# One sweep of probability-value products per step in place of two, in an audio-tower kernel

## What is computed

```
h = relu(patches @ W1 + b1) @ W2 + b2
h = h + bitlinear_attention(layernorm(h))     # 16 heads of 16
h = h + one_expert_ffn(layernorm(h))          # capacity 100
h = h + real part of a complex decaying scan(layernorm(h))
h = h + mixture_of_8_experts(layernorm(h))    # two of 8 experts for each row
```

```
scores = einsum('bhqd,bhkd->bhqk', q, k) * SCALE
attn = softmax(scores, axis=-1)
out = einsum('bhqk,bhkd->bhqd', attn, v)
```

## Time and profile before

| | |
|---|---|
| three executions | 504.51, 506.26, 506.55 us; median 506.26 us |
| the profiled execution | 505.15 us, with a span of 503.4 us |
| mean granted clock of TensorE | 0.954 of full speed |
| busy: PE, DVE, ACT, POOL | 439.5, 281.0, 206.0, 166.6 us |
| the chain that ended last | PE 65%, DVE 17% |

### The profile page before, as it was taken

How to read it: one execution, slowest core, us unless ns; L and a number is a source line. 1 busy time by engine, 2 the same in 40 slices (tenths; PEclk the granted TensorE clock), 3 DMA queues, 4 the chain that set the end, 5 groups by cost and what they waited for, 6 DMA issues and landing times.

```text
span 503.4 us, 9416 instructions
## 1 busy us (share of the span) xinstructions
PE 439.5 (87%) x3418; PEld 282.7 (56%) x3419; DVE 281.0 (56%) x853; ACT 206.0 (41%) x385; POOL 166.6 (33%) x140
## 2 busy tenths in 40 slices
PE   0889899798778856878899999999999999999991
PEld 0545456456455645646557666666666666566651
DVE  0498786686869999998975767346411111111110
ACT  1234653463587424246426632453333333333330
POOL 6051010010101044631434455443544442554322
PEclk9999999999967956898999999999999999999997
DMA  8999210046045100732005222341333225333211
GB/s 174 255 210 211 58 40 3 9 132 241 19 155 210 44 7 1 276 143 85 26 28 126 42 43 43 101 69 20 50 46 53 42 42 187 63 45 50 41 21 21
DMA packets 36103, 43.16 MB, mean 86 GB/s; under 512 B 5216, under 2 KB 30560, under 8 KB 35904
## 3 DMA queue, kind: packets, MB, share of 16 engines
q1 hardware_dynamic: 26384, 32.14, 22.9%
q0 software_dynamic: 7488, 10.23, 12.9%
q10 hardware_dynamic: 2192, 0.27, 0.5%
HBM read 30.96 MB, written 11.53 MB: 84 GB/s over the span
## 4 chain that ended last, share of the span: by engine, by line
PE 65%; DVE 17%; issue 5%; DMA 5%; ACT 4%; SPq 3%; POOLq 0%; DVEq 0%; ACTq 0%
PE psum L2257 26%; PE psum L2276 13%; PE psum L1874 9%; DMA M3s<-in_x_dram 4%; PE psum L2267 3%; PE psum L1888 3%; PE psum L1900 2%; PE psum L2247 2%; PE psum L1918 2%; DVE st_att L1028 1%; SPq L316 1%; DVE H L1271 1%; DVE qtok L1188 1%; DVE Eb L1068 1%; DMA out_dram<-O,dst_i 1%
## 5 line engine op out<-in xcount | busy, mean ns | idle before, releaser
L1771 DVE TENSOR_TENSOR QT<-QT,psum 128x512 f32<-128x512 f32 x39 | 26.8, 687 | 136.9 <-PE psum L2257 136.9
L2276 PE MATMUL psum<-M3s,KT 128*128 x312 | 74.1, 380 | 1.3 <-ACT KT L822 0.8
L2257 PE MATMUL psum<-M1s,KT 128*128 x156 | 74.0, 597 | 1.1 <-issue 0.8
L2257 PE MATMUL psum<-M2s,KT 128*128 x156 | 73.3, 592 | 0.0
L2276 PEld LDWEIGHTS psum<-M3s,KT 128*128 128x128 f32 x312 | 58.6, 190 | 22.1 <-issue 16.1
L833 ACT ACTIVATE O<-psum,gate_slot 128x256 f32<-128x256 f32 x39 | 18.5, 474 | 106.7 <-PE psum L2276 106.7
L1874 PE MATMUL psum<-M2s,M1s 128*128 128x512 f32 x128 | 58.7, 602 | 0.8 <-ACT H L688 0.7
L503 POOL DMA_INDIRECT KT<-mixture_rows_in,src_i x39 | 42.6, 1093 | 33.0 <-issue 19.7
L2257 PEld LDWEIGHTS psum<-M2s,KT 128*128 128x128 f32 x156 | 29.6, 190 | 37.3 <-issue 37.3
L530 POOL DMA_INDIRECT mixture_rows_out<-O,src_i x17 | 30.8, 1813 | 33.1 <-ACT O L833 13.3
L818 ACT ACTIVATE QT<-psum 128x512 f32<-128x512 f32 x39 | 23.3, 596 | 39.8 <-PE psum L2257 39.7
(11 more groups left out here) (407 smaller groups left out, 747.1 us busy)
## 6 DMA issues: line engine op xcount, KB each, us to landing
M3s<-in_x_dram SPq DMA_DIRECT2D x4, 1024.0 KB, 11.8
M3s<-in_L_ffn_W_dram SPq DMA_DIRECT2D x1, 4096.0 KB, 15.1
M2s<-in_L_ffn_W_dram SPq DMA_DIRECT2D x1, 4096.0 KB, 15.4
M1s<-in_L_ffn_W_dram SPq DMA_DIRECT2D x1, 4096.0 KB, 15.1
M3s<-in_x_dram SPq DMA_DIRECT2D x4, 992.0 KB, 15.7
M1s<-vtok SPq DMA_DIRECT2D x64, 34.0 KB, 1.9
mixture_rows_out<-H SPq DMA_DIRECT2D x4, 512.0 KB, 4.1
M1s<-in_L_tok_W_dram SPq DMA_DIRECT2D x2, 512.0 KB, 14.2
```

Of the source, the lines that this page charges most:

```text
L1771: v.tensor_tensor(sil[:, u, :], sil[:, u, :], bank[3], ALU.mult).then_inc(v_gated, 1)
L2257: last = mm(z, xrT[:, u, c, :], w[:, bass.ds(e, 1), c, :].rearrange("p a h -> p (a h)"), start=(c == 0), stop=(c == CH - 1))
L2276: last = mm(bank[6][:, 0:DM], actT[:, u, c, :], M3s[:, bass.ds(e, 1), c, :].rearrange("p a d -> p (a d)"), start=(c == 0), stop=(c == HC - 1))
```

## The change

There are five buffers of probabilities (`turned`): the two of `Eb`, the two of `PT` and 512 numbers of each partition of `M1s` that nothing used at that time. Batch `b` has its scores in `EB[b]` (the two of `Eb`, in turn, as before) and its transposed probabilities in `PB[b]`: `PT` 0, `PT` 1, the part of `M1s`, and for batch 3 `Eb` 0, which batch 2 has by then given up. `values` is called once for a step, over all four batches for each head, at the place of the second call.

```
+        turned = [Eb[:, 0], Eb[:, 1], PT[:, 0], PT[:, 1], part(M1s, VX_W + STRIDE * DM + CH * SN, NH * 32)]
+        turned = turned[0:4] + [turned[4].rearrange("p (h k) -> p h k", k=32)]
+        EB = [turned[k] for k in (0, 1, 0, 1)]
+        PB = [turned[k] for k in (2, 3, 4, 0)]
...
-                    a.activation(Eb[:, b % 2], Eb[:, b % 2], ACT.Exp).then_inc(a_exp, 1)
+                    a.activation(EB[b], EB[b], ACT.Exp).then_inc(a_exp, 1)
...
-            act.wait_ge(v_probsT, BT * STEPS)
+            act.wait_ge(p_values, BT * STEPS)
             norm(SR, 0, X4[0], v_norm4_in, a_norm4)
...
-            act.wait_ge(p_values, BT * STEPS)
             norm(SR, 1, X4[1], v_norm4_in, a_norm4)
...
                 wait(dve, v_probsT, BT * i + b - 1)
+                if b == 0:
+                    wait(dve, p_values, BT * i)
...
-                v.tensor_tensor(Eb[:, b % 2], score_rows(b), m, ALU.subtract).then_inc(v_less_max, 1)
+                v.tensor_tensor(EB[b], score_rows(b), m, ALU.subtract).then_inc(v_less_max, 1)
...
             def turn(i, b):
                 dve.wait_ge(a_exp, BT * i + b + 1)
-                wait(dve, p_values, BT * i + b - 1)
-                v.transpose(PT[:, b % 2].rearrange("p h k -> p (h k)"), Eb[:, b % 2].rearrange("p h k -> p (h k)")
+                wait(dve, p_values, BT * i)
+                if b == BT - 1:
+                    dve.wait_ge(v_probsT, BT * i + b)
+                v.transpose(PB[b].rearrange("p h k -> p (h k)"), EB[b].rearrange("p h k -> p (h k)")
                             ).then_inc(v_probsT, 1)
...
-            def values(i, slot, batches):
+            def values(i, slot):
...
-                pe.wait_ge(v_probsT, BT * i + batches[-1] + 1)
+                pe.wait_ge(v_probsT, BT * (i + 1))
                 for h in range(NH):
                     w = TS * VW
-                    for b in batches:
+                    for b in range(BT):
                         last = mm(bank[2 + h // 4][32 * b:32 * b + 32, w * (h % 4):w * (h % 4 + 1)],
-                                  PT[:, b % 2, h, :], Vx[:, b, :, h, :], start=True, stop=True)
-                last.then_inc(p_values, len(batches))
+                                  PB[b][:, h, :], Vx[:, b, :, h, :], start=True, stop=True)
+                last.then_inc(p_values, BT)
...
-            values(0, 2, range(0, 2))
             layer2(2)
-            values(0, 2, range(2, BT))
+            values(0, 2)
...
             att_proj(0)
-            values(1, 3, range(0, 2))
             pe.wait_ge(v_att_added, 1)
             layer2(3)
-            values(1, 3, range(2, BT))
+            values(1, 3)
...
-                if iC is not None:
-                    values(iC, slot, range(0, 2))
                 if iN is not None:
                     wait(pe, v_less_max, BT * done(slot, C_LAG))
                     wait(pe, a_norm2T, done(slot - 1, D_LAG))
                     norm3_columns(iN, bank[0:2])
                 if iC is not None:
-                    values(iC, slot, range(2, BT))
+                    values(iC, slot)
```

## The result

The changed kernel takes **506.49 us** (median of 12 runs, 504.43 to 509.85). Twelve runs of the kernel before on the same chip gave 505.16 us (504.27 to 506.55). The ratio is 1.0037, with a 95% interval of 1.0022 to 1.0052: slower by 0.37%, where 504.9 us and a small gain were forecast. The time lies within the range given, 503.0 to 507.6, but on the wrong side of no change. The profiled execution took 508.09 us at a mean granted clock of 0.937 (before: 505.15 us at 0.954). It is 1.6 us above its kernel's median, so it shows the losses larger than the median has them.

What follows compares the result with a forecast made beforehand. PE was taken to bound slots 2 and 3, DVE slots 4 and 5. Terms -1.24, -0.71, 0, +0.2 and +1.05 sum to -0.70 us, set against the 505.62 us mean: 504.9 us, range 503.0 to 507.6.

Steps and rivals of the forecast that it cites:

- Pace of the merged sweep: Each step's `values` on PE: 128 records at 15.6 ns each, so four batches take about 2.02 us, as two did.
- Rivals 2 and 3: Merged sweeps slower than forecast: no faster than two batches (511.0 us, 8%), or a pace between, 3.0 us each (506.3 us, 7%).
- rival 2: Merged sweeps: four batches run no faster than two, each sweep 2.02 us longer; 511.0 us, chance 8%.
- Slot 2, -1.24 us: Without the first sweep ahead of it, `layer2` waits only for ACT's relu and starts 1.24 us earlier, as does `att_rows`.
- Slot 3, -0.71 us: Without the first sweep, `layer2` waits for DVE's `v_att_added` and starts at 119.48 instead of 120.19 us.
- Waits, +0.2 us: Fourth transpose waits for the third on DVE: 0.1 us a step, on the path in slots 4 and 5.
- Slots 4 and 5 at 0: Merged sweep ends where the second one ended, covered by DVE's slack of 1.2 and 2.1 us: no change.
- The clock, +1.05 us: Slot 4's new PE hole halves the clock once, costing 1.7 us less 0.65 us of `att_mean`'s wait.
- a rival of 17%: Slot 3: the clock falls there too, `layer2` runs 3.4 us at half speed, +1.7 us; 506.6 us, chance 17%.
- rival 4: Clock falls in slot 3 as well as slot 4: `layer2` +1.7 us, 506.6 us in all, chance 17%.
- dearer bound: Slot 4: sweep and transposes both at half clock, costing 2.26 us instead of 1.05; with slot 3's fall, 507.8 us.

Runs made afterwards that it cites:

- e4: Changed kernel plus dummy matmuls in three PE holes: seven behind slot 2's sweep, five ahead of slot 3's `layer2`, nine in slot 4; 503.54 us, ratio 0.9973.
- e1: Changed kernel with its buffers and waits, but `values` called twice a step at the old places in all four steps; 506.12 us, ratio 1.0016.
- e11: Changed kernel with one merged sweep in slot 5 alone, two calls of `values` in the other steps; 505.90 us, ratio 1.0010.
- e10: Changed kernel with one merged sweep in slot 4 alone, two calls of `values` in the other steps; 507.44 us, ratio 1.0040.
- e12: Changed kernel with one merged sweep in slot 2 alone, two calls of `values` in the other steps; 504.20 us, ratio 0.9980.
- e9: Changed kernel without the six old dummy matmuls ahead of `att_mean` in slot 4; 506.41 us, ratio 1.0025.
- e5: Changed kernel plus nine dummy matmuls ahead of `norm3_columns` in slot 4 alone; 505.44 us, ratio 1.0004.
- e6: Changed kernel plus dummy matmuls in slots 2 and 3 only (seven behind slot 2's sweep, five ahead of slot 3's `layer2`); 504.51 us, ratio 0.9985.
- e3: Changed kernel with merged sweeps in slots 4 and 5 only, two calls of `values` in slots 2 and 3; 507.10 us, ratio 1.0037.
- e2: Changed kernel with merged sweeps in slots 2 and 3 only, two calls of `values` in slots 4 and 5; 505.29 us, ratio 1.0001.

## Why the prediction was wrong

- **Pace of the merged sweep: right.** 15.6 ns a record was forecast, 15.9 came. Rivals 2 and 3 fall. The Trainium skill's floor in "TensorE: Matmul & The Clock Gate", section "Wait — 56ns, not 53.3ns?", about 25 ns from one matmul's start to the next, would have made it 3.2 us. The trace shows 2.03, so that floor doesn't hold for these records. The prediction's figure for rival 2, that slots 2 and 3 have given their gain back at about 20 ns a record, was too low: 1.95 us over two sweeps of 128 is 7.6 ns above 15.6, so about 23.
- **Slot 2, -1.24 us: right.** -1.15 was measured, with ACT as releaser.
- **Slot 3, -0.71 us: right as a term, but not seen in the profile of the changed kernel.** `layer2` waits for DVE, as forecast. With the clock kept up (e4), slots 2 and 3 together bring 126.35 - 124.65 = 1.70 us at slot 3's `att_rows`, where 1.95 was forecast. Of that 1.12 are slot 2's and 0.58 slot 3's.
- **Waits, +0.2 us: right in size, wrong in place.** 0.1 us was forecast in each of slots 4 and 5; the profiles show 0.23 in slot 4 and nothing in slot 5. The median of e1 leaves room for more.
- **Slots 4 and 5 at 0: right for slot 5 only** (e11's profile). In slot 4, DVE's slack of 1.2 us was the cover, and half clock used it up.
- **The clock, +1.05 us: the step that failed.** The forecast allowed one fall, in slot 4, at the price of the shortest stretch, left slot 2's hole at nothing, and called a fall in slot 3 a rival of 17%. The profile shows four falls. By an estimate from the measured terms, the clock cost about 2.8 us in the median, not 1.05: the measured +1.33, plus the 1.70 gained, less the 0.23 of the wait. The three fills of e4 take back 3.0.

What they cost, worked out from the rows. *Slots 2 and 3:* the fall at 91.4 us delays `layer2` of slot 3 by 118.83 - 118.37 = 0.46 us against e4. The one at 118.7 us makes `layer2` there 124.54 - 118.83 = 5.71 us long in place of 122.46 - 118.37 = 4.09, so +1.62. The latter is what rival 4 had priced at 1.7. Together they are 2.08 us, more than the 1.70 gained, which leaves `att_rows` of slot 3 0.38 late. The sweep of scores gives 0.37 back, as told above. *Slot 4:* DVE enters it 0.01 us from where it did before (the exponentials' subtraction at 157.21 and 157.20 us), so all of the 3.27 us at `att_mean` arise inside. The sweep starts 0.25 us later (163.53 against 163.28), which is the wait of the fourth transpose, and ends after 4.30 us in place of 2.02 (`norm2_columns` at 167.83 against 165.30). The expert's rows and dummies take 4.18 us at half clock, and 2.56 at full clock in e10. That is 0.25 + 2.28 + 1.62 = 4.15, less the 0.65 us that `att_mean` used to wait: 3.5 us, near the 3.27 measured. The forecast's dearer bound, 2.26, had the sweep but not the expert's rows.

So the case that happened in the profile is rival 4 with the dearer bound, and somewhat more. That case was +2.21 us by its own sum (507.8 less 505.62). Between the two profiled executions it is +2.94. That 507.8 stands so near the 508.09 measured is luck in part, since the forecast was set on the mean of the executions of before and the profiled one was 0.5 us below it. What rival 4 lacked is the fall behind slot 2's sweep, which I had not priced, because PE had come through that hole of 2.01 us at full clock before, and the expert's rows at half clock. The hole is as long as it was (2.03 us). What changed is what stands before it: one sweep less, and a new hole of 0.78 us ahead of `layer2`. All five profiles that merge slot 2 and fill nothing there have this fall, and one of five with two calls has it (e1). So merging brings it about, but isn't the only thing that can. How it does so isn't shown. e12's profile has it too, from 91.8 us, and e12 still gained 1.1 us in the median.

The median is milder than the profile, +1.3 against +2.9 us. The falls of slots 2 and 3 and the first of slot 4 are in every profile that could have them; the second of slot 4 is in two of five. With it missing, `att_mean` came 2.1 us sooner after the start of the sweep (e10). The changed kernel's four slowest runs have mean clocks of 0.935 to 0.940 and its fastest, 504.43 us, has 0.949. That fastest run is close to the 504.9 forecast, which suggests that the forecast was about an execution with few falls. Only one execution of the changed kernel was profiled, so this isn't shown.

**The other rule of the Trainium skill,** that PE transposes don't count as busy for the clock gate as matmuls do ("TensorE: Matmul & The Clock Gate", "Part 4: PE-mode transpose"), stands untested. In this profile the clock fell at 159.7 us, in a bare hole, 1.5 us before the first transpose, so those transposes can't have brought it about. In e10, e9 and e5 the fall comes later, at 162.6, 163.0 and 164.0 us, with the eight transposes before it, which agrees with the rule, but no run isolates it.

## What to carry to other kernels

Before sparing PE work ahead of a wait for another engine, ask what becomes of the time: holes of 1 to 3 us on PE cost 2.1 us in slots 2 and 3 and about 3 in slot 4 of the profile, where the granted clock fell at them and the work behind ran at half speed on the path. Spare it where PE itself is the bound, but keep real work (or, failing that, dummies that end before the wait does) in the hole, and leave it alone where the other engine ends last anyway, as in slots 4 and 5. When a change leaves holes, read the granted clock in several executions, of before as well: one profile shows one pattern of falls out of several, and the profile of before here had lost 0.37 us to a fall of its own.

## What the runs showed of the hardware

- Full-height products of 128x32 weights and 68 columns (f32) in four column groups run at 15.9 ns a record (2.03 us for 128): 128 take as long as 64 do in two column groups (2.02 us). In e5, whose sweep is nearly all at half clock, the 128 take 3.73 us, 29 ns each.
- Dummy matmuls in holes pay: seven of them (1.6 us) delay what follows by 0.04 us, and 21 in three holes are worth 3.0 us against the same kernel without them. In the kernel before, seven of them behind slot 2's second sweep change nothing (0.9983 to 1.0005).
- Shortly after the clock came back in the middle of a sweep, PE stood still with nothing shown to wait for: 0.59 us in the changed kernel (at 166.91 us, the rise was at 166.5), 0.77 us in e6 (at 164.10) and 0.47 in e3 (at 166.69). In e9 and e10 it was 0.11 and 0.07 us. I have no explanation.
- The clock fell in 14 of the 14 merged holes that nothing filled, in 1 of 19 of the same places with two calls, and in 1 of 9 with dummies in them (the table of all fourteen profiles).
- The changed kernel's executions spread by 5.4 us (504.43 to 509.85), the slower ones mostly at a lower mean granted clock. The kernel before spreads by 2.3 us beside it, and by up to 3.4 in the larger batches. So the change also cost steadiness.
- A fall can also come where no kernel differs: in e2's profile alone the clock was at half from about 35 to 39 us, for 1.68 us.
